# Attention over edge counts: one multiplication per pair of tiles, one exponential per pair

## The reference, cut to what matters

```
h = (x @ W).reshape(n, H, C)
es = jnp.einsum('nhc,hc->nh', h, a_src)[src]
ed = jnp.einsum('nhc,hc->nh', h, a_dst)[dst]
e = jax.nn.leaky_relu(es + ed, negative_slope=0.2)
m = jax.ops.segment_max(e, dst, num_segments=n)
p = jnp.exp(e - m[dst])
z = jax.ops.segment_sum(p, dst, num_segments=n)
alpha = p / z[dst]
out = jax.ops.segment_sum(h[src] * alpha[:, :, None], dst, num_segments=n)
```

## Time and profile before

| | |
|---|---|
| median of 3 runs | 6369.94 us |
| the profiled execution | 6337.15 us |
| its span, first to last instruction | 6335.4 us |
| mean granted TensorE clock | 0.851 |
| PE, DVE, ACT busy | 70%, 49%, 33% of the span |

### The profile page before, as it was taken

One profiled execution on the slowest core, in us unless ns is written; L12 is line 12 of the kernel. 1 busy time (PEld: TensorE's weight loads), 2 busy tenths in 40 slices (PEclk: granted clock), 3 DMA queues, 4 the chain that ended last, 5 costly groups with the idle time before them and its releaser, 6 DMA issues. The chain is left out here.

```text
span 6335.4 us, 60833 instructions
## 1 busy us (share of the span) xinstructions
PE 4466.2 (70%) x18528; PEld 2931.0 (46%) x18528; DVE 3121.7 (49%) x6025; ACT 2114.8 (33%) x4133; POOL 1608.9 (25%) x1750
## 2 busy tenths in 40 slices
PE   1330037995574676869996698996685867897898
PEld 1220025774210555757775123223574545574676
DVE  8431025112787537851114997985885026444211
ACT  5100000213485104632222687884553110203122
POOL 1467761664575541100000211100111020000000
PEclk9965568998687888979998898997896988898899
DMA  9300026116344445530000444441552327361000
GB/s 379 145 1 1 1 84 191 46 38 176 108 151 144 130 137 179 176 75 0 0 0 36 150 165 127 156 144 52 193 165 83 112 70 219 102 208 31 0 0 20
DMA packets 405633, 664.34 MB, mean 105 GB/s; under 512 B 108992, under 2 KB 210360, under 8 KB 399864
## 3 DMA queue, kind: packets, MB, share of 16 engines
q1 hardware_dynamic: 368152, 654.14, 31.3%
q0 software_dynamic: 37216, 7.08, 0.7%
HBM read 542.72 MB, written 118.31 MB: 104 GB/s over the span
## 5 line engine op out<-in xcount | busy, mean ns | idle before, releaser
L1195 PE MATMUL l2g_a_agg_acc<-all_x,l2g_a_h 128*65 128x512 f32 (+1 forms) x1400 | 650.2, 590 | 23.8 <-ACT l2g_a_agg_flat L1220 21.1
L385 POOL DMA_INDIRECT far<-all_nil,all_far_cell x416 | 497.7, 1196 | 317.6 <-DMA far<-all_nil,all_far_cell 156.2
L385 POOL DMA_INDIRECT table<-first_count,first_cell x416 | 411.9, 990 | 343.8 <-issue 294.6
L1293 DVE SCALAR_TENSOR_TENSOR all_x<-all_x,l2g_a_agg_counts 128x512 f32<-128x512 f32 (+1 forms) x700 | 405.0, 627 | 121.3 <-ACT all_x L1243 120.8
L1232 ACT ACTIVATE l2g_a_agg_z<-l2g_a_agg_z 128x512 f32<-128x512 f32 (+1 forms) x700 | 344.3, 538 | 145.5 <-PE l2g_a_agg_z L1175 121.1
L853 PE MATMUL l3g_agg_acc<-l3g_agg_halves,l3g_agg_exact 128*128 128x512 f32 x1250 | 306.6, 400 | 91.9 <-DVE l3g_agg_exact L906 87.0
L1243 ACT ACTIVATE all_x<-l2g_a_agg_z 128x512 f32<-128x512 f32 (+1 forms) x700 | 353.8, 569 | 0.5 <-PE l2g_a_agg_z L1184 0.5
L385 POOL DMA_INDIRECT table<-all_count,all_cell x256 | 257.8, 1007 | 259.7 <-PEq L51 108.4
L853 PE MATMUL l0g_agg_acc<-l0g_agg_halves,l0g_agg_exact 128*128 128x512 f32 x625 | 164.3, 419 | 210.6 <-issue 199.4
L1793 DVE SCALAR_TENSOR_TENSOR all_x<-l1f_moe_py,l1f_gate,all_x 128x256 f32 x200 | 96.8, 484 | 437.1 <-PE l1f_moe_py L1750 437.1
L853 PEld LDWEIGHTS l3g_agg_acc<-l3g_agg_halves,l3g_agg_exact 128*128 128x128 f32 x1250 | 239.2, 192 | 155.1 <-DVE l3g_agg_exact L906 87.9
(11 more groups left out here) (759 smaller groups left out, 9390.2 us busy)
## 6 DMA issues: line engine op xcount, KB each, us to landing
l3g_agg_counts<-table SPq DMA_DIRECT2D x250, 320.0 KB
l2g_a_agg_counts<-table SPq DMA_DIRECT2D x300, 256.0 KB
table<-counting_eye_rows SPq DMA_DIRECT2D x25, 1600.0 KB, 38.7
l0g_agg_counts<-table SPq DMA_DIRECT2D x125, 320.0 KB
l1g_agg_counts<-table SPq DMA_DIRECT2D x125, 320.0 KB
l2g_a_agg_mask<-far SPq DMA_DIRECT2D x50, 800.0 KB
l1g_gat_agg_counts<-table SPq DMA_DIRECT2D x150, 256.0 KB
l2g_b_agg_counts<-table SPq DMA_DIRECT2D x150, 256.0 KB
```

What stands on the lines that cost most here:

```text
L385: pool.indirect_dma_start(self.table, bass.IndirectOffsetOnAxis(ap=self.cell[:, b, p:p + 1], axis=0), self.count(b, p), None, bounds_check ...
L1195: pe.matmul(to, rhs(t, r * per + h), p[:, u % n_p, 0:n], start=(t == 0), stop=(t == nt - 1), skip_group_check=True).then_inc(summed, 1)
L1293: dve.scalar_tensor_tensor(out=w, in0=w, scalar=1.0, in1=counts[:, b % n_counts, 0:n], op0=ALU.min, op1=ALU.mult).then_inc(weighted, 1)
```

## The change

In `attend_heads` ACT does the exponentials of a batch's two units in one instruction over two banks of `z`, unless the pair would wrap round the five banks (one batch in five, u % 5 = 4), and adds 2 to `exp_ready` at its end. DVE multiplies both units in one instruction, with the counts tile read twice, once both exponentials are done. On ACT the second `flatten` stands behind the pair; before it stood between the two exponentials.

In `attend` the exponentials and the multiplications of two adjacent units go together where neither ring wraps between them (`run_of`); the count ring grows from 9 to 10 tiles. In the built program ACT has these exponentials in the four-head stages: layer 2 has 240 pairs of 2 x 512, 40 of 2 x 128, 120 + 20 single; layer 0 has 102 pairs, 52 single. DVE has pairs alone there: 350 and 128. Each one-head stage has 71 pairs and 33 single ones on both engines.

```diff
--- before.py
+++ after.py
@@ -1233,16 +1233,21 @@
                                            ).then_inc(bent, 1)
                     if t == 0 and sp >= 1:
                         flatten(sp - 1, 0)
-                    for h in range(per):
-                        if b >= 1:
-                            u = (b - 1) * per + h
-                            n = batch(b - 1)[4]
-                            act.wait_ge(z_shifted, u + 1)
-                            if u >= n_p:
-                                act.wait_ge(summed, u - n_p + 1)
-                            act.activation(p[:, u % n_p, 0:n], z[:, u % nz, 0:n], ACT.Exp).then_inc(exp_ready, 1)
-                        if h == 0 and t == 0 and sp >= 1:
-                            flatten(sp - 1, 1)
+                    if b >= 1:
+                        u = (b - 1) * per
+                        n = batch(b - 1)[4]
+                        if u >= n_p:
+                            act.wait_ge(summed, u + per - n_p)
+                        if u % nz + per <= nz:
+                            act.wait_ge(z_shifted, u + per)
+                            act.activation(p[:, u % n_p:u % n_p + per, 0:n], z[:, u % nz:u % nz + per, 0:n], ACT.Exp
+                                           ).then_inc(exp_ready, per)
+                        else:
+                            for v in range(u, u + per):
+                                act.wait_ge(z_shifted, v + 1)
+                                act.activation(p[:, v % n_p, 0:n], z[:, v % nz, 0:n], ACT.Exp).then_inc(exp_ready, 1)
+                    if t == 0 and sp >= 1:
+                        flatten(sp - 1, 1)
                     if (b + 2) % nb == 0 and b + 2 < n_batches:
                         copy_tops((b + 2) // nb)
                 for h in range(per):
@@ -1286,12 +1291,12 @@
                     b = u // per
                     sp, t, r, t0, n = batch(b)
                     i = u % (nb * per)
-                    dve.wait_ge(exp_ready, u + 1)
                     if u % per == 0:
+                        dve.wait_ge(exp_ready, u + per)
                         dve.wait_ge(counts_in[b % n_counts], 16 * (b // n_counts + 1))
-                    w = p[:, u % n_p, 0:n]
-                    dve.scalar_tensor_tensor(out=w, in0=w, scalar=1.0, in1=counts[:, b % n_counts, 0:n], op0=ALU.min,
-                                             op1=ALU.mult).then_inc(weighted, 1)
+                        w = p[:, u % n_p:u % n_p + per, 0:n]
+                        dve.scalar_tensor_tensor(out=w, in0=w, scalar=1.0, in1=over_mid(counts[:, b % n_counts, 0:n], per),
+                                                 op0=ALU.min, op1=ALU.mult).then_inc(weighted, per)
                     if sp >= 1:
                         at = i - per * (lag + 4)
                         if at >= 0 and at // 6 < backs and at % 6 < 3:
@@ -1309,7 +1314,7 @@
 
     n_pad = nt * P
     table2 = table[0:n_pad * n_pad, 0].rearrange("(r n) -> r n", n=n_pad)
-    n_counts, n_p, n_mask = 9, 11, 3
+    n_counts, n_p, n_mask = 10, 11, 3
     spans = [(0, t, min(4, nt - t)) for t in range(0, nt, 4)]
     n_units = len(spans) * nt
     f = width - 1
@@ -1319,6 +1324,15 @@
 
         sp, t = divmod(u, nt)
         return sp, t, spans[sp][1], spans[sp][2]
+
+    def run_of(u):
+
+
+        t = u % nt
+        first = u - t % 2
+        if first % nt + 1 < nt and first % n_p + 1 < n_p and first % n_counts + 1 < n_counts:
+            return (first, 2) if u > first else None
+        return u, 1
 
     with Scope(nc, tag) as s:
         counts = s.sb("counts", [P, n_counts, 512])
@@ -1455,11 +1469,12 @@
                             act.wait_ge(rows_ready, 2 * sp + 2)
                         act.activation(p[:, u % n_p, 0:m * P], rows[:, sp % 2, 1, 0:m * P], ACT.Identity,
                                        bias=es2[:, t:t + 1]).then_inc(low_ready, 1)
-                    if u >= 2:
-                        m = unit(u - 2)[3]
-                        act.wait_ge(score_ready, u - 1)
-                        act.activation(p[:, (u - 2) % n_p, 0:m * P], p[:, (u - 2) % n_p, 0:m * P], ACT.Exp
-                                       ).then_inc(exp_ready, 1)
+                    if u >= 2 and run_of(u - 2) is not None:
+                        v, k = run_of(u - 2)
+                        m = unit(v)[3]
+                        act.wait_ge(score_ready, v + k)
+                        act.activation(p[:, v % n_p:v % n_p + k, 0:m * P], p[:, v % n_p:v % n_p + k, 0:m * P], ACT.Exp
+                                       ).then_inc(exp_ready, k)
                     if u % nt == nt - 6 and u + 6 < n_units:
                         copy_tops(u // nt + 1)
                     if u % nt == nt - 4 and u + 4 < n_units:
@@ -1500,12 +1515,15 @@
                     v = u - 3
                     if v >= 0:
                         sp, t, t0, m = unit(v)
-                        k = v % n_counts
-                        dve.wait_ge(exp_ready, v + 1)
-                        dve.wait_ge(counts_in[k], 16 * (v // n_counts + 1))
-                        w = p[:, v % n_p, 0:m * P]
-                        dve.scalar_tensor_tensor(out=w, in0=w, scalar=1.0, in1=counts[:, k, 0:m * P], op0=ALU.min,
-                                                 op1=ALU.mult).then_inc(weighted, 1)
+                        if run_of(v) is not None:
+                            at, k = run_of(v)
+                            dve.wait_ge(exp_ready, at + k)
+                            for i in range(at, at + k):
+                                dve.wait_ge(counts_in[i % n_counts], 16 * (i // n_counts + 1))
+                            w = p[:, at % n_p:at % n_p + k, 0:m * P]
+                            dve.scalar_tensor_tensor(out=w, in0=w, scalar=1.0,
+                                                     in1=counts[:, at % n_counts:at % n_counts + k, 0:m * P], op0=ALU.min,
+                                                     op1=ALU.mult).then_inc(weighted, k)
                         if t == 1 and sp:
                             finish(sp - 1)
                         for n in looks.after.get(v, ()):
```

## The result

The changed kernel takes 6424.43 us (median of 11 runs), the kernel before 6370.92 beside it: ratio 1.0088, interval 1.0071 to 1.0106. It is slower by 53.5 us. The forecast was +23: the sign was right and the time lies in the range (6358 to 6426), just inside its upper end, but the size is less than half of what came.

A forecast was written before the change was run, and what follows sets the result against it. The prediction took PE to have least room in layer 2, the longest window. Its terms, 28 + 5 + 3 - 7 - 5 + 2 - 3 = +23 us, gave a median of 6393 us, range 6358 to 6426.

The forecast's parts named there:

- Term A: Steady layer-2 batches: the second score waits for the paired exponential, 0.30 us late in alternate paired batches; +28 us.
- Term B: Start of a layer-2 wide span: the second copy comes 0.43 us later behind the pair, PE waits; +5 us.
- Terms C and D: Layer 2, second turning back. C: wait becomes 4.17 us, +3 undisturbed, -7 with look. D: less idle, clock falls less, -5.
- Layer 0: Layer-0 stage: ACT's steady batches 0.07 us longer, counting only in two spans not waiting for POOL; +2 us.
- One-head stages: Pause at unit 12: four earlier multiplication pairs a span bring the last look 0.28 us forward; -3 us over two stages.
- nothing alternates and the clock falls more: Rival for layer 2: each pair loses most of 0.30 us and the clock does not recover; +55 us, 6425, chance 0.12.
- Lateness was not swallowed: Denies the rival that PE absorbs the pair's lateness in layer 2: -5 to 3 us, about 6368, chance 0.26.

The follow-up runs named there:

- z4: y1 with the four-head stages' exponentials paired, multiplications still single, finish early; ratio 0.9979 to the kernel before.
- x3: The changed kernel with the four-head stages' multiplications single again, exponentials still paired; ratio 1.0032 to the kernel before.
- x4: The changed kernel with the third part of finish directly behind the second, ahead of the next paired multiplication; ratio 1.0064 to the kernel before.
- y1: The kernel before with one-head stages paired and the whole first finish behind unit 14, ahead of the look; four-head operations single; ratio 0.9905.
- x1: The kernel before with only the one-head stages changed: exponentials and multiplications paired, ten count tiles; ratio 0.998.
- v3: The kernel before with ten count tiles instead of nine in the one-head stages and nothing else; ratio 0.9998.

## Why the prediction was right or wrong

- **Term A** (+28): right in mechanism and nearly in size. 17.4 + 5.3 = 23 us in the changed kernel, 22 in z4, 0.29 late in two batches of five.
- **Term B** (+5): the pause was priced right, and what follows it was not. 4.50 for 4.07 us in the undisturbed spans is the forecast 0.43. The rest of the +10.7 is the clock, which falls behind the pause in nine of the twelve spans instead of seven. "Behind an idle 1.73 they take 2.01" was read from one span as if a pause had one price. Why the clock falls in one span and not in another is open: x3 and x4 have the same pause and only +1.0 and +1.6.
- **Terms C and D** (+3, -7, -5): the step that failed is the arrears of term C. "DVE has saved 22 x 0.07 = 1.5 by then ... DVE's arrears are gone and 4.17 holds" takes the whole lateness of the nine spans (5.0 against 3.2) for arrears that can be worked off. At most 0.37 us of it were; the rest is the look, which stands directly ahead of the units that the turning back waits for and takes 3.48 us however early DVE is. In layer 2 DVE stands idle for 166.3 us ahead of the pairs (75.0 of them put down to exponentials), so savings turn into idle time, and the order look, pair, part, pair, part gets longer by one unit. The turning back came 5.5 to 5.9 us behind the scores instead of 4.17, so the clock's 5 us were lost too: +24.0 instead of -9. x4 and y1 take it away by moving the parts. These terms alone are 33 us off, more than the 30 by which the whole is. In the spans without the look term C was right: 4.22 us.
- Two slips in their sums change little: half of 9 x 1.35 is 6 and not 5, and two spans are undisturbed and not three, since the first span has nothing to turn back. The sum would be +21.
- **Layer 0** (+2): +10.8. The stretch of GpSimd's row beside paired multiplications had no term, nor had the lower clock with paired exponentials (0.77 instead of 0.83).
- **One-head stages** (-3): -17, mis-sized. I counted only the pairs of units 2 to 11. The pause at unit 12 fell from 3.96 to

```profile
2538.83 0.66 PE L1414 MATMUL l1g_gat_agg_misc<-all_ident,l1g_gat_agg_cols 128*64 128x128 f32 x4 [2.63 <-POOLq L1404]
```

but that is not all gain. From the last instruction of `finish` to the end of the last look DVE takes 19.66 us instead of 19.93, the forecast 0.28 a span; the pause is shorter by 1.33 because PE now also waits for pairs on the way and reaches it 0.92 later. What the sum left at nothing is the stretch behind the pause: from the tops to the next `finish` PE takes 23.05 to 24.6 us instead of 24.4 to 25.7, and its busy time in the stage fell by 5 us with the same 1283 matmuls, at a clock of 0.97 for 0.96. A shorter pause gives back clock too.
- **The rivals**: "nothing alternates and the clock falls more" came nearest in size (+55) and was wrong in its mechanism: the losses do alternate, and the clock falls at the pauses. Lateness was not swallowed.

The rule that I left out is the Trainium skill's, SBUF — State Buffer, section "SBUF: two separate sides": a DVE instruction with two inputs in SBUF and a GpSimd instruction that reads SBUF contend for one pair of ports, and whichever starts first holds it for its whole instruction. The trace agrees for GpSimd's side, by 0.20, 0.54, 1.07 and 3.33 us; whether GpSimd also holds up DVE no run here was made to show.

## What to carry over

Merging two operations saved about 0.06 us a pair here and makes everything that waits for the first half, or for the engine, wait for both: look for who stands behind, a `finish` on the same queue or GpSimd beside it, before counting the saving. Whether a saving on an engine is worth anything is asked at the place where it is last; an engine that waits ahead of its long instruction has no arrears to work off. The best place for short work that another engine waits for is ahead of the long one: moving three short parts ahead of a look took 39 us from layer 2 (x1's 810.1 to y1's 771.4) and about 45 from the time, more than any pair brought.

## What the runs showed of the hardware

A pause costs PE more than its length. The granted clock is 0.60 of full speed, a mean of its two levels, over the sums behind the 3.35 us pause of the changed kernel, and 1.00 in the next batch:

```profile
3717.86:3720.90 3.04, 3.04 (x8) 0.75 (x4) 0.85 (x1) 2.00 (x3) 0.00 (x0) 0.60 0.00 0
3721.25:3723.10 1.85, 1.85 (x8) 0.47 (x4) 1.85 (x2) 1.75 (x3) 0.00 (x0) 1.00 0.00 0
```

Of the 32 us that x4 gained in layer 2, 12 are PE's idle time and 20 its busy time. But a pause has no fixed price: the same 1.73 us came with 2.01 us of sums in one span and 3.33 in another. And the same program differs by 2.6% between chips (6372 and 6207 us). That difference lies ahead of everything treated here: the multiplications of layer 0 start at 1673.1 us in the kernel before and at 1546.0 in v3, 127 of the 130 us by which the two profiles differ.
